# Loads by graph, three block buffers, later reciprocals, a new order for the first graph and paired negations in a graph attention kernel

## The reference

```python
q, k, v = (proj(Wq, bq), proj(Wk, bk), proj(Wv, bv))
scores = jnp.einsum('bhqd,bhkd->bhqk', q, k) * SCALE
mask = (adj_matrix + bond_matrix)[:, None, :, :]
attn = jax.nn.softmax(scores * mask, axis=-1)
ctx = jnp.einsum('bhqk,bhkd->bhqd', attn, v)
x = _layernorm(x + (ctx @ Wo.T + bo), axis=-1)
```

## Time and profile before

| | value |
|---|---|
| median of three runs | 437.6 us |
| the profiled execution | 432.45 us |
| its span in the trace | 430.8 us |
| busy: VectorE, TensorE, ScalarE, GpSimd | 90%, 89%, 84%, 58% |
| granted TensorE clock | 0.997 of full speed |
| bytes moved by DMA | 92.28 MB, mean 214 GB/s |

### The profile page before, as it was taken

One profiled execution on the slowest core, in us unless ns is written; L12 is line 12 of the kernel. 1 busy time (PEld: TensorE's weight loads), 2 busy tenths in 40 slices (PEclk: granted clock), 3 DMA queues, 4 the chain that ended last, 5 costly groups with the idle time before them and its releaser, 6 DMA issues.

```text
span 430.8 us, 12136 instructions
## 1 busy us (share of the span) xinstructions
PE 383.4 (89%) x3628; PEld 291.0 (68%) x3628; DVE 387.9 (90%) x1592; ACT 360.5 (84%) x1223; POOL 249.6 (58%) x379
## 2 busy tenths in 40 slices
PE   8968999998989899998999999899898999997682
PEld 6755767776767676675777667677766767775452
DVE  4687999999999999999899999989999999999965
ACT  4588899888888888888988888899888789988760
POOL 3330656748385664748567474856747385554455
PEclk9999999999999999999999999999999999999998
DMA  8548869788887978878797888889788787978632
GB/s 288 168 107 217 235 165 304 175 265 217 232 242 181 303 159 252 247 202 263 192 295 182 243 242 210 254 203 294 178 251 228 163 256 178 276 170 214 155 90 73
DMA packets 58658, 92.28 MB, mean 214 GB/s; under 512 B 7777, under 2 KB 47970, under 8 KB 58594
## 3 DMA queue, kind: packets, MB, share of 16 engines
q1 hardware_dynamic: 45266, 66.35, 60.8%
q10 hardware_dynamic: 13328, 25.17, 16.9%
HBM read 26.22 MB, written 8.39 MB: 80 GB/s over the span
## 4 chain that ended last, share of the span: by engine, by line
ACT 31%; PE 20%; DVE 16%; SPq 12%; issue 11%; DMA 7%; POOL 1%; ACTq 0%; DVEq 0%; POOLq 0%
ACT probs L705 24%; SPq L202 8%; DVE probs L502 8%; PE ctx_bank L396 5%; DMA v_boxed<-v 5%; DVE boxes L520 5%; PE proj_bank L325 4%; PE out_bank L343 4%; SPq L211 4%; PE row_bank L256 3%; ACT turned_probs L713 3%; ACT inverse L719 2%; PE turn_bank L273 1%; ACT kq L733 1%; DVE top L502 1%
## 5 line engine op out<-in xcount | busy, mean ns | idle before, releaser
L705 ACT ACTIVATE probs<-probs,low_top 128x256 f32<-128x256 f32 x512 | 254.7, 504 | 41.5 <-DVE low_top L511 40.4
L502 DVE CUSTOM_DVE_ANT_0 probs<-row_bank,adj_rows 128x256 f32<-128x256 f32 x512 | 188.0, 416 | 5.1 <-PE row_bank L256 4.8
L520 DVE STREAM_TRANSPOSE boxes<-probs 128x1536 f32<-128x1536 f32 x62 | 109.7, 1769 | 1.0 <-DMA carried<-boxes 1.0
L705 ACT ACTIVATION_READ_ACCUMULATOR probs<-probs,low_top 128x1 f32 x512 | 99.3, 194 | 0.0
L325 PE MATMUL proj_bank<-xt_parts,w_parts 128*128 128x512 f32 x360 | 99.3, 411 | 0.0
L325 PEld LDWEIGHTS proj_bank<-xt_parts,w_parts 128*128 128x128 f32 x360 | 63.0, 188 | 30.2 <-issue 19.6
L256 PE MATMUL row_bank<-kq 32*128 32x256 f32 x1024 | 73.3, 400 | 5.2 <-DVE top L502 3.9
L396 PE MATMUL ctx_bank<-carried,v_boxed 128*32 128x256 f32 x744 | 59.5, 382 | 19.1 <-DMA v_boxed<-v 16.1
L842 POOL COPY wide<-shares 128x512 f32<-128x512 f32 x32 | 19.5, 610 | 74.9 <-DVE shares L528 74.9
L396 PEld LDWEIGHTS ctx_bank<-carried,v_boxed 128*32 128x32 f32 x744 | 31.2, 109 | 43.5 <-issue 30.7
L413 PE MATMUL out_bank<-w_parts,ctx_parts 128*128 128x256 f32 x372 | 51.5, 287 | 9.9 <-issue 6.7
(11 more groups left out here) (85 smaller groups left out, 467.2 us busy)
## 6 DMA issues: line engine op xcount, KB each, us to landing
carried<-boxes SPq DMA_DIRECT2D x248, 192.0 KB, 4.0
adj_rows<-in_adj ACTq DMA_DIRECT2D x16, 512.0 KB, 6.6
xr<-in_x ACTq DMA_DIRECT2D x16, 512.0 KB, 6.9
v_boxed<-v SPq DMA_DIRECT2D x124, 64.0 KB, 2.5
out<-result ACTq DMA_DIRECT2D x31, 256.0 KB, 4.8
xt<-in_x_t SPq DMA_DIRECT2D x15, 512.0 KB, 4.2
xt<-in_x_t SPq DMA_DIRECT2D x2, 256.0 KB, 3.2
w_whole<-in_wk ACTq DMA_DIRECT2D x2, 128.0 KB, 3.4
```

Source lines behind the costliest of these rows:

```text
L502: last = nc.vector.tensor_tensor_reduce(probs[:, h % RING, t * S:(t + 1) * S], row_bank[j][:, t * S:(t + 1) * S], adj_rows[:, (g // 2) % 2 ...
L520: nc.vector.transpose(boxes[:, n % 2].rearrange("p a h (f q) -> p (h f) a q", q=D), probs[:, first:first + BOXED, :].rearrange("p h (f a k ...
L705: last = nc.scalar.activation(tile, tile, ACT.Exp, bias=low_top[:, g % 2, J * c + j, t:t + 1], accum_out=sums[:, g % 2, t, j * T + c:j * T ...
```

## The change

Five things. (1) adj, x and x_t are loaded by graph or by half instead of by pair: 256 KB a DMA instead of 512 KB, with a semaphore each. ScalarE's queue issues adj of graph g+2 after its third head and x of graph g after its seventh, in each step; x_t comes in its two halves, one in each step. (2) There are three buffers for blocks, so `box` waits for the blocks of group n-3. (3) `divide` of a graph is called behind the second head of the next graph's first group. (4) The first graph: TensorE does keys and queries, then v(0), then the second group's scores ahead of the rest, and makes the bias in step 1; VectorE reads the first query tile ahead of cutting the v weights; ScalarE's copies in step 0 move to other heads. (5) `lower_top` becomes `lower_tops`: one instruction negates the maxima of two heads, behind the third head and behind the fourth.

```diff
+BOXES = 3
...
-        boxes = sb("boxes", [P, 2, J, BOXED, P])
+        boxes = sb("boxes", [P, BOXES, J, BOXED, P])
...
-            def load_x_t(pair):
+            def load_x_t(pair, t):
                 if pair == 2:
-                    sp.wait_ge(first_low, T)
-                wait(sp, xt_low, T * (pair - 2))
-                sp.dma_start(xt[:, pair % 2].rearrange("p t s -> p (t s)"), x_t[pair]).then_inc(xt_in[pair % 2], 16)
+                    sp.wait_ge(first_low, t + 1)
+                if pair > 2:
+                    sp.wait_ge(xt_low, T * (pair - 3) + t + 1)
+                sp.dma_start(xt[:, pair % 2, t, :], x_t[pair][:, t * 2 * S:(t + 1) * 2 * S]).then_inc(xt_in[pair % 2][t], 16)
...
-                if g % 2 == 1 and is_pair(g // 2 + 4):
-                    load_x_t(g // 2 + 4)
+                if g > 0 and is_pair((g + 1) // 2 + 3):
+                    load_x_t((g + 1) // 2 + 3, (g + 1) % 2)
...
             rows(0)
+            for half_ in range(2):
+                project_kq(1, 0, half_)
             project_v(0)
-            make_bias()
+            rows(1)
+            for half_ in range(2):
+                project_kq(1, 1, half_)
+            project_v(1)
+            turn_probs(0)
...
-            def lower_top(n, j):
-                g, place = n // T, J * (n % T) + j
-                dve.wait_ge(rows_used, J * n + j + 1)
-                nc.vector.tensor_reduce(low_top[:, g % 2, place, :], top[:, g % 2, place, :].unsqueeze(2), AXIS.X, ALU.max,
-                                        negate=True).then_inc(top_ready, 1)
+            def lower_tops(n, half_):
+
+                g, place = n // T, J * (n % T) + 2 * half_
+                dve.wait_ge(rows_used, J * n + 2 * half_ + 2)
+                nc.vector.tensor_reduce(low_top[:, g % 2, place:place + 2, :], top[:, g % 2, place:place + 2, :].unsqueeze(3),
+                                        AXIS.X, ALU.max, negate=True).then_inc(top_ready, 2)
...
-                wait(dve, carried_in[n % 2], 64 * (n // 2))
+                if n >= BOXES:
+                    dve.wait_ge(carried_in[(n - BOXES) % 4], 64 * ((n - BOXES) // 4 + 1))
...
+            read_first_q(0)
             low_weights(2)
-            for c in range(T):
-                read_first_q(c)
+            read_first_q(1)
...
                 for j in range(J):
                     reduce_rows(n, j)
-                    if j > 0:
-                        lower_top(n, j - 1)
-                lower_top(n, J - 1)
+                    if j == 2:
+                        lower_tops(n, 0)
+                    if j == 1 and n % T == 0 and n > 0:
+                        divide(n // T - 1)
+                lower_tops(n, 1)
...
-                if 0 <= g < LAST:
-                    divide(g)
...
-                    if s == 1 and g % 2 == 0 and is_pair(ahead):
-                        load_masks(ahead)
+                    if s == 2 and is_graph(g + 2):
+                        load_masks(g + 2)
...
-                    if s == 2 and g % 2 == 0 and is_graph(g):
-                        load_x(g // 2)
+                    if s == 6 and is_graph(g):
+                        load_x(g)
```

More of the change, by code:

```diff
@@ L100, in build @@
         biases_in = sem("biases_in")
-        xt_in, x_in, adj_in, stored, carried_in, v_in = (
-            [sem(f"{name}{n}") for n in range(2)] for name in ("xt_in", "x_in", "adj_in", "stored", "carried_in", "v_in"))
+        stored, v_in = ([sem(f"{name}{n}") for n in range(2)] for name in ("stored", "v_in"))
+        x_in, adj_in, carried_in = ([sem(f"{name}{n}") for n in range(4)] for name in ("x_in", "adj_in", "carried_in"))
+        xt_in = [[sem(f"xt_in{n}_{t}") for t in range(T)] for n in range(2)]
         xt_first = [sem(f"xt_first{t}") for t in range(T)]
@@ L213, in carry_v @@
                                  ).then_inc(v_in[n % 2], 16)
-            load_x_t(1)
+            for t in range(T):
+                load_x_t(1, t)
             for n, dram in ((2, wv), (3, wo)):
@@ L219, in _ @@
                 sp.dma_start(tile[:], dram).then_inc(biases_in, 16)
-            load_x_t(2)
-            load_x_t(3)
+            for pair in (2, 3):
+                for t in range(T):
+                    load_x_t(pair, t)
             carry_v(0)
@@ L377, in weigh_v @@
                     pe.wait_ge(moved, 2 * g + 2)
-                    for c in range(T):
-                        pe.wait_ge(carried_in[c], 64 * (g + 1))
+                    for n in range(T * g, T * g + T):
+                        pe.wait_ge(carried_in[n % 4], 64 * (n // 4 + 1))
                 for half_ in range(2):
@@ L458, in step @@
                         project_kq(ahead, 2 * (g % 2), half_)
+                if g == 1:
+                    make_bias()
                 if is_graph(g - 2):
@@ L492, in reduce_rows @@
                 h = J * n + j
-                if h % (4 * J) == 0 and h % (2 * H) == 0:
-                    dve.wait_ge(adj_in[(g // 2) % 2], (g // 4) * 16 + 16)
+                if h % H == 0:
+                    dve.wait_ge(adj_in[g % 4], (g // 4) * 16 + 16)
                 if j < BOXED:
@@ L690, in _, with load_masks, load_x @@
         def _(act):
[L691 to L698, removed]
+            def load_masks(g):
+                wait(act, rows_used, H * (g - 3))
+                act.dma_start(adj_rows[:, (g // 2) % 2, g % 2].rearrange("p t s -> p (t s)"),
+                              adj[g // 2][:, (g % 2) * T * S:(g % 2 + 1) * T * S]).then_inc(adj_in[g % 4], 16)
+            def load_x(g):
+                wait(act, y_ready, g - 3)
+                act.dma_start(xr[:, (g // 2) % 2, g % 2].rearrange("p t e -> p (t e)"),
+                              x[g // 2][:, (g % 2) * T * E:(g % 2 + 1) * T * E]).then_inc(x_in[g % 4], 16)
             def exp(n, j):
@@ L828, in cut_x @@
             def cut_x(pair, t):
+                pool.wait_ge(xt_in[pair % 2][t], 16 * loads(pair))
                 if t == 0:
-                    pool.wait_ge(xt_in[pair % 2], 16 * loads(pair))
                     wait(pool, v_made, 2 * pair - 2)
@@ L854, in add_bias @@
             def add_bias(pair, b):
[L855 to L858, removed]
+                if pair == 0 and b == 0:
+                    pool.wait_ge(bias_ready, 1)
+                pool.wait_ge(x_in[2 * (pair % 2) + b], (pair // 2) * 16 + 16)
                 tile = xr[:, pair % 2, b]
```

19 lines of the change are left out of this document (12 added, 7 removed).

## The result

The changed kernel takes 421.04 us (median of six runs, 416.9 to 424.25) against 436.89 us for the kernel before on the same chip (median of six, 435.11 to 439.08). That is 15.85 us less by the medians, where 21.6 us had been forecast; the range of 408 to 427 us holds it. Executions fall in a faster and a slower state, and the ratio is formed from the faster ones alone, without the changed kernel's 424.25 us (the profiled execution) and 424.16 us: 0.9603, 95% interval 0.9548 to 0.9658, faster by 4%, where 0.951 had been forecast. A second profiled execution of the changed kernel took 422.81 us; where no block is late, its step is the same 12.07.

A forecast was written before the change was run, and what follows sets the result against it. It took the ring between VectorE's reciprocal and ScalarE's exponentials, 12.24 us, plus 0.26 of late blocks, as the bound. A step of 11.86 saves 19.2 us and the first graph 2.4: 437.6 - 21.6 = 416.0 us, range 408 to 427.

The forecast's parts named there:

- The reciprocal's ring: VectorE's reciprocal, ScalarE's exponentials and back: 12.24 us a step before, 11.56 with the reciprocal behind two heads of masks.
- the signs that were to show the rest right: ScalarE's first-head wait under 0.8, VectorE 94% or more, boxes 11.7 to 12.0 apart, graph 1's first exponential near 25.9.
- a step over 12.2 with VectorE idle: Sign that the prediction is wrong: a step above 12.2 us while VectorE idles, whatever it waits for.
- What is late next: Next step limit: VectorE's work 11.80, 11.66 with paired negations, ahead of TensorE's 11.57 and the ring's 11.56.
- Paired negations: VectorE, 4 negations a graph instead of 8: saves 0.14 us a graph (0.14 to 0.28).
- It adds nothing to ScalarE's first exponential: Moved reciprocal with pairing: two heads earlier by the wait, one head later by the pairing, so no delay in itself.
- Loads by graph: Smaller, spread loads of adj, x and x_t: free all of the 0.26 us a step, or none.
- the 0.26 a step: Time over the ring's 12.24 in the 12.50 step before, put down to TensorE waiting for carried blocks every second step.
- "nothing" for the x_t halves on SyncE's queue: One more DMA issue every second step, behind the v carries and ahead of the block carries: cost taken as nothing.
- The Trainium skill's rule of 1 MiB loads: Batch DMAs to 1 MiB or more for 75% of peak; behind the rival of small loads filling DMA engines, chance 0.07.
- The first graph: New order at the start: first exponential near 14.17, reciprocal 1.6 us sooner, 0.85 more after it; 2.4 us together.
- The sum: 11.86 a step, 19.2 us over 30 steps, plus 2.4: 21.6 off; the median kept 5.15 above the profiled execution.

The follow-up runs named there:

- part 3 alone: The reciprocals behind the second head of the next graph's masks, with single negations, added to the kernel before: 436.98 us, ratio 0.9937.
- parts 2 to 5: The changed kernel with adj, x and x_t loaded by pair again, 512 KB a DMA, at the heads and steps of before: 428.42 us, ratio 0.9778.
- the experiment: The changed kernel with the first graph's order as before: 421.89 us, ratio 0.9663; graph 1's first exponential at 27.33.

## Why the prediction was right, and where not

**The reciprocal's ring: right.** 12.24 as worked out; without the change of place and with pairing 12.92 forecast, 12.93 measured. Its wait is gone.

Of the signs that were to show the rest right, none came: ScalarE's wait at a graph's first head is 1.0 (under 0.8 asked for), VectorE's share 90% (94%), graph 1's first exponential at 26.60 (25.9), the step 12.26 to 12.30. One of the signs of being wrong did come, "a step over 12.2 with VectorE idle".

**What is late next: this step failed.** I summed each engine's own work (11.66, 11.57) and the known ring (11.56) and took the longest. The loop that decided was none of them: it runs over three engines through a shared PSUM bank. Its terms could have been added up from the timelines, nearly all of them from those of before: 5.00 from the first exponential to the end of the fourth head's copies, 0.10, 1.66 of projection, then residual, transpose, statistics, two heads, the reciprocal, a third head and the negation. It is 12.07, and 0.41 over the 11.66 is 12 us in 30 steps. In the kernel before, with single negations, it was shorter by the third head's 0.68, an estimate of 11.4, and hidden under 12.24; it is the pairing that lifted it over the engines' own work. The 11.66 itself was good: 11.71 measured.

**Paired negations: wrong in sign, twice.** The sum took 0 for the negation at a group's end, which has to wait for the last accumulator; it costs 0.10 there, so VectorE's step grows by 0.07 with the pairing (11.64 to 11.71) and does not shrink by 0.14. And "It adds nothing to ScalarE's first exponential" held only for the ring that I had in view. With single negations the kernel was no slower (0.9534 against 0.9603 and 0.9653), and its mean step was 12.01.

**Loads by graph: right in kind, mis-sized.** The sum kept 0.20 of the 0.26 a step, so the part was worth 1.8 us in it, with 7.8 as its upper bound; undone, it costs 7. The waits for blocks fell from 19.0 to 11.7 us; they are not alike in every step and not under 0.5, as I had asked for. What I did not see is how much the parts need each other: part 3 alone gave 0.6%, parts 2 to 5 gave 2.2%, all five 3.5 to 4%. And "nothing" for the x_t halves on SyncE's queue was wrong: in the longest step of either profile the chain runs through one of them (last section). The Trainium skill's rule of 1 MiB loads (DMA: Bandwidth & Descriptors, section Bandwidth) did not hold against it here: halving the loads made the kernel faster. What the rule says of a single load shows in part, as x_t lands in a median of 3.7 us for 256 KB against 4.2 for 512 KB, while adj takes 4.7 against 6.6. No load here had 1 MiB.

```profile
xt<-in_x_t SPq DMA_DIRECT2D x32, 256.0 KB, 3.7
adj_rows<-in_adj ACTq DMA_DIRECT2D x32, 256.0 KB, 4.7
```

**The first graph: mis-sized.** Forecast 2.4 us, measured 28.25 - 26.60 = 1.65, of which the order itself is 0.7 to 0.8 by the experiment. The first exponential came at 15.01 and not near 14.17. The cut of the v weights stands between the two query tiles now and took 1.62 us, so VectorE came to the second tile at 12.11, where the kernel before had it at 11.06, and to the first masks, behind it, at 12.77, where it had been 12.60. The earlier tile gave nothing, and the pairing took its 0.7.

```profile
10.56 1.62 DVE L629 TENSOR_TENSOR w_parts<-w_whole,w_parts 128x512 fp32r<-128x512 f32 x1
12.11 0.74 DVE L636 TENSOR_SCALAR kq<-turn_bank,b_q 128x512 f32<-128x512 f32 x1
```

**The sum.** 11.86 a step against 12.30 (12.26 in the second profile). By the two profiled executions of the first pair that is only 8.2 us, by the medians 15.85: the profiled execution of before (432.45) was faster than all of the six runs behind its median, so its 12.50 flatters the kernel before, and the constant 5.15 that I carried over was not constant. That error ran against the other, and this is luck: the forecast was 5 us off, and not 13. With the measured steps (0.20 to 0.24 less than 12.50) and the 1.65 of the first graph, the prediction's own sum gives 429 to 430 us, outside its range.

## What to carry to other kernels

When a wait that closes a ring is taken away, don't look for the next limit in the engines' sums alone: follow every buffer or bank that two kinds of work share, and add up the loop from one engine's first instruction back to itself, for the order of instructions as it will be. Merging small instructions can save their cost and delays the first result by what they wait for; where a ring passes through that first result, leave it single, and read the saving from the distance between starts, since busy time showed one here where there was none. And try a part alone before judging it: the spread loads and the third buffer were worth little by the waits of before, but without the other parts the moved reciprocal gave next to nothing.

## What the runs showed of the hardware that was not expected

**A long stand of TensorE can cost more than its length.** In the changed kernel one weighing waited 2.45 us for blocks. The rows are that weighing, the transposes behind it (they usually take 0.66), and the stretch from 187 to 190 us, with the granted clock ahead of the DMA share and GB/s at its end.

```profile
185.82 1.57 PE L404 MATMUL ctx_bank<-carried,v_boxed 128*32 128x256 f32 x18 [2.45 <-DMA v_boxed<-v]
...
188.63 1.12 PE L281 MATMUL turn_bank<-ident,probs 128*128 128x128 f32 x4
```

```profile
187.00:190.00 3.00, 3.00 (x23) 1.92 (x16) 1.26 (x2) 0.88 (x5) 0.50 (x1) 0.50 0.96 246
```

The clock was 0.50, which is the lower of its two levels, 1.2 for 2.4 GHz. From the weighing's start to the scores' (191.30) it is 5.48 us, against 3.88 in the step of 259.27 to 263.15: 1.6 us lost on top of the 2.45. It happened three times in this execution, behind stands of 1.99, 2.45 and 2.10, and once in the second one, behind a stand of 2.89 and again in a step of 15.82. The length of the stand doesn't decide alone. A stand of 1.67 at 285.13 left the clock alone, but so did one of 2.09 in the kernel before, at 389.58, and in the changed kernel's two executions the same stand, of 1.99 and 2.00, was followed by the lower clock in the first (the scores behind took 2.09) and by the full clock in the second (1.15):

```profile
32.80 0.86 PE L281 MATMUL turn_bank<-ident,probs 128*128 128x128 f32 x4 [1.99 <-ACT inverse L743]
```

```profile
32.69 0.63 PE L281 MATMUL turn_bank<-ident,probs 128*128 128x128 f32 x4 [2.00 <-ACT inverse L743]
```

So the same kernel pays for it in one execution and not in another. Over the changed kernel's first six executions, 416.9 to 424.25 us, the mean clock lies between 0.984 (the slowest) and 0.995 (the fastest), though not in order in between. Whether keeping TensorE busy through such a wait would hold the clock was not tried.

**A queue that waits holds up what stands behind it.** The 2.45 us did not start at the DMA engines. The chain that ended last, followed in order of time, goes through an x_t load on SyncE's queue: the load waited for GpSimd to finish with the half that it overwrites, its turn took 1.86 us where it usually takes 0.58, and the carries of the blocks were issued one after the other behind it.

```profile
169.80 1.32 POOL xt_parts L862
171.12 1.48 SPq L199
174.74 2.86 SPq L208
...
182.97 2.84 DMA v_boxed<-v
185.82 2.88 PE ctx_bank L404 x32
```

In the second execution the chain to the stand of 2.89 us goes through an x_t load too, one that took 1.73. Issuing x_t behind the carries, or from another queue, was not tried.
